# A graph layer and a ternary feed-forward network: the residual of nine tiles moved to GpSimd, and the first units' steps in another order

## The chip, the cores and the metric

One core of one Trainium2 chip runs the whole program. The metric is the device time of one execution in microseconds (us). The kernel before takes 344.32 us, the median of three runs (343.66 to 345.22). TensorE is called PE below, VectorE DVE, ScalarE ACT, GpSimd POOL and SyncE SP.

## The reference

```python
x = x + gnn(layernorm(x), src, dst, W_self, W_neigh, b)     # x: 1250 x 512
x = x + ffn(layernorm(x), w_gate, w_up, w_down)

def gnn(x, ...):      # 20000 edges, sorted by dst
    neigh = segment_sum(x[src], dst) / max(degree, 1)
    h = x @ W_self + neigh @ W_neigh + b
    h = where(h >= 0, h, 0.01 * h)
    return h / max(norm(h, axis=1), 1e-12)

def ffn(x, ...):      # weights ternary: sign times mean(|w|) of each group of 128
    h = silu(x @ gate.T) * (x @ up.T)                        # 1408 wide
    return h @ down.T
```

## The kernel before, in words

The 1250 nodes are ten tiles of 125 rows (`NT = 10`, `TP = 125`). Every engine runs a list of its own, in the order in which it is written, and they wait for each other by semaphores alone. There are three stages.

Stage 1 (to 112 us) normalizes x, multiplies it by the two weights, builds the 1250 x 1250 matrix of edge counts `a_t` from one-hot columns, and makes ternary signs of 25 of 34 blocks of weights.

Stage 2 is the loop `for n in range(NT)` on PE, DVE and ACT. PE adds up the neighbours of tile n in bank 4 + n % 2 (L1336: 20 products, `y_hi` and `y_lo` for each of ten source tiles). DVE takes the bank (`neighbour_sum`, L1121), applies the leaky slope (`leak`, L1127), and a tile later inverts the norm and adds the scaled tile to x (`residual`, L1130 to L1144, with the statistics for the second layernorm). ACT squares and sums the row (L876), takes the roots (L878, L831) and writes the normalized tile `xn` (`normalize1`, L837). PE transposes it after the sum n of tile n - 3 (L1349), ACT copies the result to `x1_hi` (L845), and DVE puts the rest into `x1_lo` (`x1_low`, L1157). Between these, ACT (`abs_of`, L768), POOL (`scales_of`, L658) and DVE (`ternary_of`, L987) make the signs of the last nine blocks: 4, 7, 4, 7, 4, 7 groups beside the tiles 0 to 5. POOL has first added the bias to all ten tiles (L698). `x1_lo` lies over `z`, the tiles that the residual reads.

Stage 3 is the feed-forward network in 33 units: one of 11 blocks of 128 hidden columns by one of three groups of tiles (376, 376 and 500 nodes). A unit has 12 pieces of two products each (L1405): G0 to G3 (gate), U0 to U3 (up), D0 to D3 (down); the D pieces follow three units behind (`LAG = 3`). Seven banks go round (`RING`): a piece waits until the piece seven before it has been taken. ACT takes G0, U0, D1 and D3 (L893), DVE the other eight (L1194). Silu is ACT's (L914), the product with up and the low part of h are POOL's (L721, L730). The eighth bank serves the transposes of signs (T) and of the tiles 7, 8 and 9 (X), at the places listed in `BANK7`. The signs of block f in use lie in `t_gu`, over the start of `a_t`, so that block 0 can't be written there before the last sum.

Of the kernel before, what the change touches and what calls it, by code (L numbers as in the profile page):

```python
# [27 lines left out]
F32R = mybir.dt.float32r  # L28
# [15 lines left out]
def gnn_ffn(nc, x, src, dst, w_self, w_neigh, bias, w_gate, w_up, w_down, out):  # L44
# [132 lines left out]
    eps = small("eps", [P, 1], F32)  # L177
    iota = small("iota", [P, 512], U16)
# [5 lines left out]
    tmp = small("tmp", [P, NCP], F32)  # L184
    flag = small("flag", [P, 1], I32)
# [22 lines left out]
    with ExitStack() as ctx:  # L208
# [134 lines left out]
        inv_done = sem("inv_done")  # L343
        x1_done = sem("x1_done")
# [11 lines left out]

        def down_jobs(n):

            lo, hi = (LOADS1 + max(0, min(NL, 3 * i // 2)) for i in (n, n + 1))
            return range(load_end[lo - 1], load_end[hi - 1])  # L360
# [42 lines left out]
        RING = [2, 6, 4, 5, 3, 1, 0]  # L403
# [18 lines left out]
        BANK7 = {(0, "U2"): ("T", 1, 0), (0, "U3"): ("X", 7), (1, "U2"): ("X", 8), (1, "U3"): ("T", 0, 1), (2, "U1"): ("X", 9),  # L422
# [10 lines left out]
        events = [("T", 0, 0)] + [BANK7[e] for e in sorted(BANK7)]  # L433
# [21 lines left out]
        t_done = sem("t_done")  # L455

# [159 lines left out]
        def _(pool):  # L616
# [79 lines left out]
            for t in range(NT):  # L696
                pool.wait_ge(z_out, t + 1)
                nc.gpsimd.tensor_tensor(z[:, t, :], z[:, t, :], bias_b[0:TP, :], ALU.add).then_inc(z_done, 1)  # L698
            for l in range(LOADS1, len(loads)):
                scales_of(l)  # L700

            nc.gpsimd.tensor_scalar(nscale[:], absum[:], 1.0 / P, Q_EPS, ALU.mult, ALU.add).then_inc(nscales, 1)
# [39 lines left out]
        def _(act):  # L742
# [105 lines left out]
            def ternary_out(f, down):  # L848
# [8 lines left out]
                if 2 <= f < NF - 1:  # L857

                    act.wait_ge(piece_ready, index[last_of[f - 2], "D0" if down else "U3"] + 1)
                if not down:  # L860
                    nc.scalar.activation(t_gu[:, t_slot[f], :, :].rearrange("p a d -> p (a d)"), source,  # L861
                                         ACT.Sign).then_inc(t_done, 1)
                else:
                    nc.scalar.activation(t_d[:, t_slot[f], :], source, ACT.Sign).then_inc(t_done, 1)


            for n in range(NT):
                if n == NT - 1:
                    act.wait_ge(n_ready, NT)
                    ternary_out(0, 0)  # L870
# [8 lines left out]
                if n >= 1:  # L879
# [14 lines left out]

            for n in range(NU + LAG):
                if n < NU:
# [7 lines left out]
                if n == 0:  # L904
                    normalize1(NT - 2)
                    ternary_out(1, 0)
                    x1_high(7)
# [7 lines left out]
                if n == 1:  # L915
                    x1_high(8)
                    normalize1(NT - 1)
                if n == 2:
                    x1_high(9)
                for what in ("D1", "D2", "D3"):  # L920
# [11 lines left out]
                    if what == "D2" and 1 <= n <= NU:  # L932
                        act.wait_ge(h_done, u + 1)
                        if u >= h_slots:
                            act.wait_ge(piece_ready, index[u - h_slots, "D0"] + 1)
                        nc.scalar.activation(h_hi[:, u % h_slots, 0:wu], hh_of(u), ACT.Copy).then_inc(hhi_done, 1)  # L936
                if n == 1:
                    ternary_out(0, 1)
                elif n in (3, 4) and (n, "U3") in BANK7:
# [14 lines left out]
        def _(dve):  # L954
# [175 lines left out]
            def residual(t, between=None):  # L1130
# [5 lines left out]
                if between is not None:  # L1136
                    leak(between)
                dve.wait_ge(inv_done, 2 * t + 2)
                nc.vector.scalar_tensor_tensor(out=x_sb[:, t, :], in0=z[:, t, :], scalar=inv[0:TP, t:t + 1],  # L1139
                                               in1=x_sb[:, t, :], op0=ALU.mult, op1=ALU.add).then_inc(x1_done, 1)  # L1140
                dve.wait_ge(x1_done, t + 1)
# [12 lines left out]
            def x1_low(t):  # L1154
                dve.wait_ge(xhi_done, t + 1)
                c, o, n = place_of(t)
# [3 lines left out]
            for n in range(NT):  # L1160
                neighbour_sum(n)
                if n >= 1:
                    residual(n - 1, between=n)
                else:
                    leak(n)
                if n >= 2:
                    shift1(n - 2)
                if n >= 3:
                    x1_low(n - 3)
                for j in down_jobs(n - 1):  # L1170
                    ternary_of(j)
                if n == 2:
                    inverse_degrees(DEG[2][0], DEG[2][1], 3, 2)
            shift1(NT - 2)
# [29 lines left out]
            for n in range(NU + LAG):  # L1204
                for what in TURN:
                    u = n - LAG if what[0] == "D" else n
                    if 0 <= u < NU and not by_act(u, what):
                        take(u, what)
                    if n == 1 and what == "U1":
                        shift1(NT - 1)  # L1210
# [7 lines left out]
                if n == 0:  # L1218
                    residual(NT - 1)
# [211 lines left out]
```

## Time and profile before

| | us |
|---|---|
| median of three runs | 344.32 |
| the profiled execution | 343.44 |
| its span in the trace | 341.7 |
| PE busy | 322.2 (94%) |
| DVE busy | 300.1 (88%) |
| ACT busy | 238.7 (70%) |
| POOL busy | 168.1 (49%) |

The span is what the trace covers, and 1.74 us of the profiled execution lie around it. Busy time is an average over the three stages. PE's first sum of stage 2 begins at 112.31 us, its first piece of stage 3 at 168.51 us.

### The profile page before, as it was taken

The numbers are of one execution on the slowest core, as the hardware profiler recorded it, in microseconds if no ns is written. First come the engines' busy times: TensorE is split into PE (matmuls) and PEld (weight loads), VectorE is DVE, ScalarE is ACT, GpSimd is POOL, SyncE is SP. The second block draws the span as 40 slices with busy tenths as digits, with TensorE's granted clock in tenths as the row PEclk, the third lists the DMA queues.
The fourth block names the chain that finished last, engine by engine and source line by source line (L and its number), as shares of the span: only waits on it lengthen the run. The fifth ranks groups of instructions, "written<-read, shape, count | busy, mean of one in ns | idle before, by whom it ended". The sixth has DMA issues, their size and how long they took to land.

```text
span 341.7 us, 5781 instructions
## 1 busy us (share of the span) xinstructions
PE 322.2 (94%) x1551; PEld 241.9 (71%) x1551; DVE 300.1 (88%) x782; ACT 238.7 (70%) x639; POOL 168.1 (49%) x234
## 2 busy tenths in 40 slices
PE   7999999999998999999969999999999999999991
PEld 3443545544543577777749898989989998899981
DVE  3899998998886348999799999999999999999993
ACT  2288987888985146784678876868768697676760
POOL 6034100000000870010006496889899897899992
PEclk9999999999999999999998999999999999999998
DMA  7982222132332002111001111111110100000305
GB/s 224 304 220 66 61 61 69 58 96 89 87 85 62 3 1 60 56 44 26 16 16 26 24 26 26 28 25 28 28 26 13 24 4 1 3 0 1 121 2 180
DMA packets 23550, 19.57 MB, mean 57 GB/s; under 512 B 15200, under 2 KB 16024, under 8 KB 23516
## 3 DMA queue, kind: packets, MB, share of 16 engines
q1 hardware_dynamic: 23438, 19.11, 20.1%
q8 instruction: 13, 0.21, 0.3%
q14 instruction: 21, 0.17, 0.1%
q10 hardware_dynamic: 78, 0.08, 0.1%
HBM read 13.73 MB, written 2.56 MB: 48 GB/s over the span
## 4 chain that ended last, share of the span: by engine, by line
PE 47%; DVE 13%; issue 4%; POOL 3%; ACT 1%; DVEq 0%; POOLq 0%; ACTq 0%
PE bank L1405 37%; PE bank L1336 6%; DVE tq_d L987 2%; POOL acc L711 2%; DVE bn L1142 2%; DVE x_sb L1139 2%; PE bank L1294 2%; DVE z L1121 1%; DVE z L1127 1%; DVE x_lo L1157 1%; PE bank L527 1%; PE bank L1322 1%; POOL h_lo L730 1%; DVE u_acc L1194 1%; DVE acc L1194 0%
## 5 line engine op out<-in xcount | busy, mean ns | idle before, releaser
L1405 PE MATMUL bank<-x_hi,t_gu 128*128 128x376 f32 (+1 forms) x264 | 94.7, 359 | 1.5 <-ACT t_gu L861 0.8
L1405 PE MATMUL bank<-x_lo,t_gu 128*128 128x376 f32 (+1 forms) x264 | 93.8, 355 | 0.0
L1294 PE MATMUL bank<-w_sb,xnT 128*125 128x512 f32 x160 | 83.0, 606 | 1.1 <-DMA w_sb<-in_L_gnn_W_neigh 0.6
L1194 DVE SCALAR_TENSOR_TENSOR g_acc<-bank,nscale,g_acc 128x376 f32<-128x376 f32 (+1 forms) x99 | 64.0, 647 | 4.6 <-PE bank L1405 3.6
L1194 DVE SCALAR_TENSOR_TENSOR u_acc<-bank,nscale,u_acc 128x376 f32<-128x376 f32 (+1 forms) x99 | 63.8, 645 | 0.0
L711 POOL TENSOR_TENSOR acc<-acc,d_one 128x376 f32<-128x376 f32 (+1 forms) x58 | 63.7, 1105 | 0.0
L658 POOL TENSOR_SCALAR thr<-absum 128x4 f32<-128x4 f32 (+1 forms) x34 | 9.1, 267 | 107.1 <-ACT mag_early L768 81.5
L721 POOL TENSOR_TENSOR hh<-sg,u_acc 128x376 f32<-128x376 f32 (+1 forms) x32 | 35.2, 1100 | 43.6 <-ACT sg L914 43.5
L1405 PEld LDWEIGHTS bank<-x_hi,t_gu 128*128 128x128 f32 x264 | 50.3, 191 | 6.3 <-issue 1.0
L1405 PEld LDWEIGHTS bank<-x_lo,t_gu 128*128 128x128 f32 x264 | 50.4, 191 | 3.4
L1246 PEld LDWEIGHTS bank<-hot_dst,hot_src 128*125 128x125 bf16 x157 | 20.7, 136 | 42.5 <-DVE hot_dst L1086 28.7
L1405 PE MATMUL bank<-h_hi,t_d 128*128 128x376 f32 (+1 forms) x132 | 47.4, 359 | 0.2
L1405 PE MATMUL bank<-h_lo,t_d 128*128 128x376 f32 (+1 forms) x132 | 46.6, 353 | 0.0
L1336 PE MATMUL bank<-y_hi,a_t 125*125 125x512 f32 x100 | 40.1, 401 | 0.8 <-DVE a_t L1043 0.8
L1194 DVE SCALAR_TENSOR_TENSOR acc<-bank,nscale,acc 128x376 f32<-128x376 f32 (+1 forms) x62 | 39.4, 643 | 0.3 <-PE bank L1405 0.3
L1336 PE MATMUL bank<-y_lo,a_t 125*125 125x512 f32 x100 | 39.5, 395 | 0.0
L730 POOL TENSOR_TENSOR h_lo<-hh,h_hi 128x376 fp32r<-128x376 f32 (+1 forms) x32 | 35.2, 1100 | 3.1 <-ACT h_hi L936 2.5
L893 ACT ACTIVATE d_one<-bank,nscale 128x376 f32<-128x376 f32 (+1 forms) x58 | 34.8, 604 | 1.7 <-PE bank L1405 1.7
L1086 DVE TENSOR_SCALAR hot_dst<-iota_w,key 128x140 bf16<-128x140 uint16 (+4 forms) x150 | 34.6, 272 | 1.2 <-PE bank L1246 1.1
L768 ACT ACTIVATE mag_early<-raw 128x128 f32<-128x128 f32 x99 | 29.6, 302 | 8.4 <-DVE tq_gu L987 6.7
L893 ACT ACTIVATE g_acc<-bank,nscale 128x376 f32<-128x376 f32 (+1 forms) x33 | 20.1, 608 | 16.5 <-PE bank L1405 15.8
L987 DVE SCALAR_TENSOR_TENSOR tq_gu<-mag_early,thr,raw 128x128 bf16<-128x128 f32 x88 | 28.8, 352 | 2.4 <-POOL thr L658 2.3
(142 smaller groups left out, 550.6 us busy)
## 6 DMA issues: line engine op xcount, KB each, us to landing
raw<-in_L_ffn_w_gate SPq DMA_DIRECT2D x11, 256.0 KB, 2.7
raw<-in_L_ffn_w_up SPq DMA_DIRECT2D x11, 256.0 KB, 2.6
out_x<-x_sb SPq DMA_DIRECT2D x10, 224.0 KB
raw<-in_L_ffn_w_down SPq DMA_DIRECT2D x8, 256.0 KB, 2.6
turned<-tq_gu SPq DMA_TRANSPOSE x80, 2.4
w_sb<-in_L_gnn_W_neigh SPq DMA_DIRECT2D x1, 1024.0 KB, 5.8
w_sb<-in_L_gnn_W_self SPq DMA_DIRECT2D x1, 1024.0 KB, 6.6
x_sb<-in_x SPq DMA_DIRECT2D x2, 448.0 KB
```

The lines of the kernel that those rows point to most:

```text
L711: nc.gpsimd.tensor_tensor(to, to, d_one[:, o, slot, 0:width(u)], ALU.add).then_inc(d_added, 1)
L721: nc.gpsimd.tensor_tensor(hh[:, u % 2, 0:w], sg[:, u % 2, 0:w], u_acc[:, u % 2, 0:w], ALU.mult).then_inc(h_done, 1)
L730: nc.gpsimd.tensor_tensor(h_lo[:, u % h_slots, 0:w], hh[:, u % 2, 0:w], h_hi[:, u % h_slots, 0:w].bitcast(F32), ALU.subtract).then_inc(hlo ...
L768: nc.scalar.activation(mag_of(j), raw_of(j), ACT.Abs, accum_out=absum[:, j:j + 1]).then_inc(abs_done, 1)
L893: nc.scalar.activation(to, bank_of(u, what)[:, 0:width(u)], ACT.Copy, scale=nscale[:, j:j + 1]).then_inc(act_took, 1)
L987: nc.vector.scalar_tensor_tensor(out=tq_of(j), in0=mag_of(j), scalar=thr[:, j:j + 1], in1=raw_of(j), op0=ALU.is_gt, op1=ALU.mult).then_inc ...
L1086: nc.vector.tensor_scalar(to, numbers, key[:, c:c + 1], None, ALU.is_equal).then_inc(hot_made, 1)
L1194: nc.vector.scalar_tensor_tensor(out=to, in0=bank_of(u, what)[:, 0:w], scalar=nscale[:, j:j + 1], in1=to, op0=ALU.mult, op1=ALU.add).then_ ...
L1246: nc.tensor.matmul(bank[k % 3][0:TP, 0:NT * WIN].rearrange("p (s d) -> p s d", d=WIN)[:, :, lo:hi], hot_src[:, c // SB % SBS, c % SB, 0:TP ...
L1294: last = nc.tensor.matmul(to[0:TP, :], xnT[:, t, k * TP:(k + 1) * TP], w_sb[:, k, half * D:(half + 1) * D], start=k == 0, stop=k == KD - 1)
L1336: last = nc.tensor.matmul(bank[4 + n % 2][0:TP, :], a_t[:, s, n * TP:(n + 1) * TP], y[:, s, :], start=s == 0 and y is y_hi, stop=s == NT - ...
L1405: last = nc.tensor.matmul(bank_of(u, what)[:, 0:width(u)], w, parts[h], start=h == 0, stop=h == 1)
```

## The change

Each part below is one of the edits.

- The residual of all tiles but tile 8 goes from one instruction of DVE to two of POOL: z times the inverse norm in place, then x plus z. POOL adds the bias to three tiles ahead of its loop and to tile t + 3 inside it; then come the scales of the tile's blocks of weights, and then the residual.
- DVE's loop has another order: `x1_low(n - 3)` comes first, then neighbour_sum, leak, the statistics of tile n - 1, the ternary groups, and only then the inverse norm of tile n and the shift of tile n - 1. `x1_low` also waits for the residual of the tile of `z` that it overwrites (`z_under`: tile 2 for the tiles 0 to 2, tile 5 for 3 to 5, 8 for 6, and 9 for 7 to 9).
- ACT normalizes tile n - 1 in its step n, after the absolute values, where it normalized tile n - 2 before them. At the last step it normalizes tile 8, copies tile 7 and takes the first two pieces before it squares tile 9.
- PE transposes tile n - 3 in the middle of the sum n. Tile 7 is transposed ahead of the first piece; the tiles 8 and 9 follow (2, G0) and (3, G0).
- The signs of block 0 go to `t_gu0`, over edge data that is no longer read. They are transposed after the sum of tile 7 and written in ACT's step 8.
- The ring of banks has another order, and in the units 0 to 2 tile 9's inverse norm, statistics, normalizing and the first h_hi have other places.

```diff
+    t_gu0 = place("t_gu0", [P, 2, D], F32R, "small", edge_data)
-        RING = [2, 6, 4, 5, 3, 1, 0]
+        RING = [2, 6, 4, 1, 0, 5, 3]
@@ pool
+            for t in range(3):
+                add_bias(t)
+            for t in range(NT):
+                if t + 3 < NT:
+                    add_bias(t + 3)
+                for l in down_loads_in(t):
+                    scales_of(l)
+                if l_done[t]:
+                    nc.gpsimd.tensor_scalar(nscale[:], absum[:], 1.0 / P, Q_EPS, ALU.mult, ALU.add).then_inc(nscales, 1)
+                if t != NT - 2:
+                    pool.wait_ge(inv_done, 2 * t + 2)
+                    nc.gpsimd.tensor_scalar(z[:, t, :], z[:, t, :], inv[0:TP, t:t + 1], None, ALU.mult).then_inc(h_unit, 1)
+                    pool.wait_ge(h_unit, min(t, NT - 2) + 1)
+                    nc.gpsimd.tensor_tensor(x_sb[:, t, :], x_sb[:, t, :], z[:, t, :], ALU.add).then_inc(x1_done, 1)
@@ scalar, in the loop over tiles
                 if n >= 3:
                     x1_high(n - 3)
+                if n == NT - 1:
+                    normalize1(NT - 2)
+                    x1_high(7)
+                    take_first()
...
-                if n >= 2:
-                    normalize1(n - 2)
...
                 for j in down_jobs(n):
                     abs_of(j)
+                if n == NT - 2:
+                    ternary_out(0, 0)
+                if 1 <= n < NT - 1:
+                    normalize1(n - 1)
+                if n == NT - 2:
+                    root_of(NT - 2)
@@ vector
             def x1_low(t):
                 dve.wait_ge(xhi_done, t + 1)
+                dve.wait_ge(x1_done, z_under(t) + 1)
...
             for n in range(NT):
+                if n >= 3:
+                    x1_low(n - 3)
+                if n == NT - 1:
+                    shift1(NT - 2)
                 neighbour_sum(n)
+                leak(n)
+                if 1 <= n < NT - 1:
+                    statistics1(n - 1)
                 for j in down_jobs(n - 1):
                     ternary_of(j)
+                if n < NT - 1:
+                    inverse_norm(n)
+                if 1 <= n < NT - 1:
+                    shift1(n - 1)
+                if n == NT - 2:
+                    residual(n)
+                    statistics1(n)
@@ vector, in the units
+                    if n == 0 and what == "G2":
+                        inverse_norm(NT - 1)
                     if n == 1 and what == "U1":
+                        statistics1(NT - 1)
+                        x1_low(7)
                         shift1(NT - 1)
-                if n == 0:
-                    residual(NT - 1)
-                    x1_low(7)
@@ tensor
+                    if s == NT // 2 and 3 <= n:
+                        t = n - 3
+                        if t >= 2:
+                            pe.wait_ge(xlo_done, t - 1)
+                        transpose_xn(t, normed1, x1_bank(t), x1n_T, place_of(t)[2])
...
-                if n == NT - 2:
+                if n == NT - 3:
                     pe.wait_ge(rdeg_done, 4)
                     ternary_in(0, 0)
...
+            through_bank7(("X", 7))
             for i, (u, what) in enumerate(pieces):
```

## Rows read from the trace of the kernel before

**Rows 1.** Chain that ended last, 112 to 190 us: start, us, what.
```profile
161.54 0.62 PE bank L1235 x4
...
162.61 4.71 PE bank L1336 x20
```
**Rows 2.** Waits of PE, 112 to 190 us: total, times, longest.
```profile
PE bank L1235 <- DVE x_lo L1157: 2.5, 1, 2.5
PE bank L1235 <- ACT xn L837: 1.2, 3, 0.5
```
**Rows 3.** Timeline of PE: start, us, instruction, idle before.
```profile
168.51 0.41 PE L1405 MATMUL bank<-x_hi,t_gu 128*128 128x376 f32 x1 [0.78 <-ACT t_gu L861]
...
178.74 0.51 PE L1405 MATMUL bank<-x_lo,t_gu 128*128 128x376 f32 x1
...
184.67 0.33 PE L1405 MATMUL bank<-h_hi,t_d 128*128 128x376 f32 x1
```
**Rows 4.** Timeline of DVE, one tile of stage 2.
```profile
146.33 0.74 DVE L1121 SCALAR_TENSOR_TENSOR z<-bank,rdeg,z 125x512 f32<-125x512 f32 x1
146.99 0.14 DVE L1133 TENSOR_SCALAR nrm<-nrm 125x1 f32<-125x1 f32 x1
...
147.25 0.67 DVE L1127 SCALAR_TENSOR_TENSOR z<-z 125x512 f32<-125x512 f32 x1
147.83 0.75 DVE L1139 SCALAR_TENSOR_TENSOR x_sb<-z,inv,x_sb 125x512 f32<-125x512 f32 x1
148.62 0.69 DVE L1142 BATCH_NORM_STATS2 bn<-x_sb 125x6 f32<-125x512 f32 x1
...
149.44 0.13 DVE L1149 RECIPROCAL rs<-sd 125x1 f32<-125x1 f32 x1
...
149.69 0.68 DVE L1157 TENSOR_TENSOR x_lo<-bank,x_hi 128x504 fp32r<-128x504 f32 x1
150.28 1.13 DVE L987 SCALAR_TENSOR_TENSOR tq_d<-mag_late,thr,raw 128x128 bf16<-128x128 f32 x4
151.32 0.75 DVE L1121 SCALAR_TENSOR_TENSOR z<-bank,rdeg,z 125x512 f32<-125x512 f32 x1
```
**Rows 5.** Timeline of ACT, the same tile.
```profile
147.95 0.60 ACT L876 ACTIVATE bank<-z 125x512 f32<-125x512 f32 x1 [0.47 <-DVE z L1127]
...
149.81 0.81 ACT L837 ACTIVATE xn<-x_sb,shift,rs 125x512 f32<-125x512 f32 x1
150.53 0.29 ACT L768 ACTIVATE mag_late<-raw 128x128 f32<-128x128 f32 x1
...
152.58 0.57 ACT L845 ACTIVATE x_hi<-bank 128x500 fp32r<-128x500 f32 x1
```
**Rows 6.** Groups of POOL by shape: busy us, mean ns, idle before.
```profile
L698 POOL TENSOR_TENSOR z<-z,bias_b 125x512 f32<-125x512 f32 x10 | 12.9, 1329 | 9.1 <-issue 9.1
...
L702 POOL TENSOR_SCALAR nscale<-absum 128x132 f32<-128x132 f32 x1 | 0.7, 698 | 0.1
...
L677 POOL TENSOR_SCALAR win_hi<-win_hi 128x157 f32<-128x157 f32 x1 | 0.6, 602 | 0.0
...
L625 POOL IOTA iota<- 128x512 uint16 x1 | 0.6, 559 | 0.0
```
**Rows 7.** Timeline of DVE and POOL where both work on SBUF.
```profile
118.10 1.12 DVE L1127 SCALAR_TENSOR_TENSOR z<-z 125x512 f32<-125x512 f32 x1
...
118.64 1.74 POOL L698 TENSOR_TENSOR z<-z,bias_b 125x512 f32<-125x512 f32 x1
```
**Rows 8.** Timeline of DVE, ACT and POOL, first units of stage 3.
```profile
172.25 0.61 DVE L1194 SCALAR_TENSOR_TENSOR g_acc<-bank,nscale,g_acc 128x376 f32<-128x376 f32 x1 [0.60 <-ACT g_acc L893]
...
177.81 1.28 ACT L914 ACT_TABLE_LOAD   x1
...
179.70 1.00 POOL L721 TENSOR_TENSOR hh<-sg,u_acc 128x376 f32<-128x376 f32 x1 [25.96 <-ACT sg L914]
```
**Rows 9.** Busy time of PE, PEld, DVE, ACT, POOL in a stretch, PE clock, DMA.
```profile
180.00:185.00 5.00, 5.00 (x26) 4.85 (x26) 4.65 (x10) 4.37 (x10) 2.89 (x4) 0.79 0.12 25
```

More of the change, by code:

```diff
@@ L177, in gnn_ffn @@
     eps = small("eps", [P, 1], F32)
+    edge_data = used["small"]
     iota = small("iota", [P, 512], U16)
@@ L343, in gnn_ffn @@
         inv_done = sem("inv_done")
+        h_unit = sem("h_unit")
         x1_done = sem("x1_done")
@@ L355, in gnn_ffn, with down_loads_in @@
         NL = len(loads) - LOADS1
+        def down_loads_in(n):
+            lo, hi = (LOADS1 + max(0, min(NL, 3 * i // 2)) for i in (n, n + 1))
+            return range(lo, hi)
         def down_jobs(n):
-            lo, hi = (LOADS1 + max(0, min(NL, 3 * i // 2)) for i in (n, n + 1))
-            return range(load_end[lo - 1], load_end[hi - 1])
+            ls = down_loads_in(n)
+            return range(load_end[ls.start - 1], load_end[ls.stop - 1])
+        l_done = [len(loads) - 1 in down_loads_in(n) for n in range(NT)]
         UNITS = [(0, 0), (0, 1), (1, 0), (1, 1), (0, 2), (1, 2)]
@@ L455, in gnn_ffn, with gate_up, z_under @@
         t_done = sem("t_done")
+        def gate_up(f):
+            return t_gu[:, t_slot[f], :, :] if f else t_gu0
+        def z_under(t):
+            c, o, n = place_of(t)
+            return (((C0[c] + CN[c]) * KD - CN[c] + o + n) * 4 - 1 - GAP) // (D * 4)
         def sg_of(u):
@@ L886, in _ @@
                     abs_of(j)
-            def take(u, what, to):
-                if took[u, what] == 1:
-                    act.wait_ge(nscales, 1)
-                act.wait_ge(piece_ready, index[u, what] + 1)
-                j = job_of(u, what)
-                nc.scalar.activation(to, bank_of(u, what)[:, 0:width(u)], ACT.Copy, scale=nscale[:, j:j + 1]).then_inc(act_took, 1)
+                if n == NT - 2:
[4 more added lines that the diff above has]
+                    root_of(NT - 2)
             for n in range(NU + LAG):
-                if n < NU:
+                if 0 < n < NU:
                     w = width(n)
@@ L931, in _ @@
                         ternary_out(*BANK7[n - 1, "U3"][1:])
[L932 to L937, printed above, removed]
+                    if what == "D2" and 2 <= n <= NU:
+                        high_of_h(u)
+                if n == 2:
                     ternary_out(0, 1)
+                    x1_high(9)
                 elif n in (3, 4) and (n, "U3") in BANK7:
@@ L1128, in leak, with inverse_norm @@
                                                op0=ALU.mult, op1=ALU.max).then_inc(leaky, 1)
-            def residual(t, between=None):
+            def inverse_norm(t):
                 dve.wait_ge(norms, t + 1)
@@ L1135, in residual @@
                 nc.vector.reciprocal(inv[0:TP, t:t + 1], nrm[0:TP, t:t + 1]).then_inc(inv_done, 1)
-                if between is not None:
-                    leak(between)
+            def residual(t):
                 dve.wait_ge(inv_done, 2 * t + 2)
@@ L1160, in _ @@
             for n in range(NT):
[L1161 to L1167, printed above, removed]
                 if n >= 3:
                     x1_low(n - 3)
+                if n == NT - 1:
+                    shift1(NT - 2)
+                neighbour_sum(n)
+                leak(n)
+                if 1 <= n < NT - 1:
+                    statistics1(n - 1)
                 for j in down_jobs(n - 1):
                     ternary_of(j)
+                if n < NT - 1:
+                    inverse_norm(n)
+                if 1 <= n < NT - 1:
+                    shift1(n - 1)
+                if n == NT - 2:
+                    residual(n)
+                    statistics1(n)
                 if n == 2:
                     inverse_degrees(DEG[2][0], DEG[2][1], 3, 2)
-            shift1(NT - 2)
             def take(u, what):
```

52 lines of the change are left out of this document (27 added, 25 removed).

## The prediction

> **What bounds the kernel now.** I read the chain of waits first. Between 112 and 161 us it runs mostly through DVE, and the sum of a tile on PE takes 4.71 us when it isn't held up [rows 1]. The transposes after it take 0.35 us more, so PE could do a tile in 5.06 us. The waits of PE come next: in stage 2 it waited three times for a normalized tile, 1.2 us in all (with the gaps that lie around these waits, 1.7 us), then 0.8 us for the signs of block 0 [rows 3], and 2.5 us for `x1_low` of tile 7 [rows 2]. From 184.67 us, the first D piece, to the tail its timeline shows no gap. So what the change can move is where that piece starts: the first G piece starts at 168.51 us, the first D piece at 184.67 [rows 3], and the rest of the program follows at PE's pace, untouched by the diff but for the names of the banks.
>
> The timeline of DVE says what a tile costs it in stage 2 [rows 4], start to start: sum 0.66, inverse norm 0.26, leak 0.58, residual 0.79, statistics 0.82, shift 0.25, `x1_low` 0.59, and 0.26 for each ternary group, 1.05 for four and 1.83 for seven. That is 5.0 and 5.8 us in turn, 5.4 in the mean: DVE, not PE, sets the pace of these tiles, and it never stands still between them.
>
> **What the change removes.** DVE loses 0.79 us a tile, which leaves it 4.2 and 5.0 us, under PE's 5.06. The 0.8 us for the signs goes, for they are ready before the last sum. Moving a transpose into the sum costs PE nothing more. If nothing else happened, the sums would end at 167.3 + 0.35 (tile 6's transposes now lie before that end) - 1.7 = 166.0 us, and the unit start would gain some 3 us more, because ACT takes the first two pieces ahead of tile 9's square. That is the ceiling: 4.5 us.
>
> **What it adds: a loop between DVE and ACT.** In the new order the last thing that DVE does for a tile is the shift; ACT's normalize waits for it (0.82 us), behind it on ACT stands `x1_high` (0.57 us) [rows 5], and the first thing of DVE's next step, `x1_low`, waits for that. Nothing of DVE can pass, the next `neighbour_sum` included. So DVE idles 0.82 + 0.57 and the handoffs, about 1.5 us, in every tile from 3 on, where it idled not at all. Its period becomes 4.2 + 1.5 = 5.7 and 5.0 + 1.5 = 6.5 us beside ternary groups, and 4.7 without. Before, `x1_low` stood behind the next tile's work, which hid ACT's part.
>
> **What it adds: POOL in the chain.** POOL starts the residual of tile n only after ACT's absolute values of the same tile, for the scales stand before it, and after DVE's inverse norm, which stands behind the ternary groups. From statistics(n - 1): 0.9, root 0.25, absolute values 4 or 7 by 0.293 = 1.2 or 2.05 (seven of them lie between 150.53 and 152.58) [rows 5], scales 0.2, scale z, add x. The add is 1.25 to 1.29 us by the bias adds [rows 6]. The multiply by a column of scalars is not in the trace. From the one-operation row, 157 columns in 0.60 us, with 0.2 us of it as the start of an instruction (what the four-column scales cost), it is 0.2 + 512 x 2.6 ns = 1.5 us; from the two-operation row, 132 columns in 0.70 us, 2.2 us [rows 6]; from below, a pass over 512 columns that reads nothing (iota) takes 0.56 [rows 6]. I take 1.5, the row with one operation. The leg is then 5.3 or 6.2 us with the handoffs, and not faster than the first loop.
>
> Beside POOL, DVE's passes with two SBUF inputs slow down: the leak at 118.10 took 1.12 us instead of 0.59, and the bias add under it 1.74 instead of 1.29 [rows 7, 4]. POOL was idle in stage 2 before, and is busy for 4 us of each tile now; I charge up to 0.5 us to each leak and add that meet, and as much again for the groups under a bias add. The Trainium skill has a rule that speaks against this change (GPSIMD Engine Reference, Key points): GpSimd shares its SBUF interfaces with VectorE, and contends with instructions that read two SBUF inputs. These two rows agree. The same page (Elementwise, side-by-side cycle accounting) has 512 elements of a tight one-input loop in 769 ns; the rows of 0.60 and 0.70 us for 157 and 132 columns are far from it. By that price my sum below would be 8.4 us instead of 11.0. Nothing else here uses it.
>
> **The two together.** `x1_low` of tile 0 now waits for the residual of tile 2, and that of tile 3 for the residual of tile 5, since it writes over them. There the legs do not overlap but follow each other, and tile 5's also has the 0.70 us of L702 in front. I wrote the four queues one below the other with these durations. The same done for the old order gives the end of the sums at 167.3, the first take of DVE at 172.2 and the first D piece at 184.2, against 167.34, 172.25 and 184.67 in the trace. For the new one:
> - Residual 2 ends at 138.9; `neighbour_sum` 3 can only start at 139.5, 4.6 us after its sum was ready.
> - PE's stalls: 0.4 us for that bank, then in the middle of the sums 5, 6 and 7 for normalized tiles 2, 3 and 4: 2.3, 1.9 and 1.8.
> - Residual 5 starts at 158.9, after nscale, and ends at 161.8; DVE has stood still since 157.0. PE loses 1.2 us for the bank and 2.3 for tile 5 in the sum 8.
> - Sum of the stalls 9.9 us, against 1.7: the sums end at 167.3 + 0.35 + 8.2 = 175.9.
> - Tile 7 is normalized only at 178.0, DVE's first take is at 181.9 (172.25 before [rows 8]): 9.7 us late.
> - Then eight takes of 0.52 and the inverse norm; statistics 9 wait for POOL to 186.7, ready 187.6; root 0.3, table 1.28 and silu 0.5 to 189.8; POOL's product 1.0 [rows 8]; two ACT takes, normalize 9 and h_hi to 192.6; POOL's h_lo and next product to 194.6; ACT's h_hi and the signs 1.1. First D piece 195.7, 11.0 us after the 184.67 of the trace.
>
> Here the change gives back nothing of what it lost; the silu of unit 0 now waits behind the root of tile 9, as it did, but the root waits for POOL. The rest keeps its length. 341.7 + 11.0 = 352.7 us of span, 354.4 with the 1.74 around it; the median of the runs lies 0.9 above the profiled execution, so I forecast 355.3. The ends: a multiply of 0.56 us gives 7.7 (352.0), one of 2.2 gives 15.2 (359.5).
>
> **Rivals.**
> - *POOL is always in time.* If the multiply is short and contention small, only the loop of DVE and ACT is left. Laid out the same way, without the waits of `x1_low` for residuals, without contention and with a short multiply of 0.8 us, the sums end at 169.4 and the first D piece at 188.8: 4.6 us, 348.9 us. For it: POOL has 5 us a tile. Against: it waits for the absolute values first.
> - *The clock falls.* After the 2.5 us stop before 178.08 us a product of 376 columns took 0.51 us instead of 0.33 [rows 3], and the granted clock was 0.79 in 180 to 185 us [rows 9]. Five stops of about 2 us in the sums, and one before the first piece, can do that again. In the sums the lateness of DVE hides most of it; at the sum 9 and the first units it does not: 2 to 4 us more, 358 us.
> - *The other side: faster.* If ACT has `x1_high` done before DVE comes to `x1_low`, DVE needs only 4.2 and 5.0 us a tile, PE sets the pace, and the ceiling of 4.5 us is had: 339.8. It decides at DVE's arrival at `x1_low`: its step must end over 1.5 us before the next sum is ready. With 5.06 us of PE and 5.0 of DVE in three of six tiles there is no such room, but the first tiles have some: the sums 0 and 1 end 7 and 5.7 us apart. If POOL then needed less than 1 us, the slack might last.
>
> **Chances.** The forecast 0.56 (its own range 351.5 to 359.5), POOL in time 0.16, the clock 0.15, faster 0.09, and 0.04 for gains and losses that cancel. Measurement can tell 0.5% here, 1.7 us: faster 0.09, same 0.04, slower 0.87. The range of 8 in 10 is 348 to 359.5 us.
>
> **What would show it.** In the profile after: idle time of DVE before L1157's line with ACT x_hi as its end, about 1.5 us a tile, and two longer ones (2.5 and 4.8 us) ended by POOL; PE idle in the middle of the sums 5 to 8, ended by ACT xn; POOL's multiply near 1.5 us; leaks of over 1 us; the last sum's end near 176 us. It is wrong if DVE's idle time before `x1_low` is under 0.5 us a tile, or if the sums end before 169 us.

## The result, and the profile after

The changed kernel takes 358.77 us, the median of four runs (358.03 to 360.55), against 344.15 us (343.66 to 345.22) for the kernel before in the same job: a ratio of 1.0428, interval 1.038 to 1.0475. The profiled execution took 359.23 us with a span of 357.5 us, 15.8 us more than before.

Three stretches make up the 15.8 us. From the first sum to the first D piece it is 85.7 us (113.30 to 198.99), against 72.4 (112.31 to 184.67): 13.3 us more. From there to the end of the span it is 158.5 us, against 157.0: 1.5 more. The first sum starts 1.0 us later, which tells nothing: the changed kernel and the eleven below, whose stage 1 is the same, start it between 112.05 and 115.83 us.

First the waits of stage 2 and of the first units, 112 to 215 us: total, times, longest.

```profile
PE bank L1288 <- ACT xn L869: 11.1, 7, 2.4
DVE x_lo L1204 <- ACT x_hi L877: 8.9, 6, 2.1
DVE x_lo L1204 <- POOL x_sb L734: 7.2, 2, 4.3
PE bank L1459 <- ACT t_d L896: 2.5, 1, 2.5
```

Before, DVE never waited at `x1_low`, and PE waited 1.2 us for normalized tiles [rows 2]. Now DVE stands still for 16.1 us before `x1_low`, and what it does next is late for PE. Of the 16.1 us, 14.2 lie in stage 2: 7.2 for POOL (tiles 0 and 3) and 7.0 for `x_hi` (tiles 1, 2, 4, 5 and 6). The sixth wait for `x_hi`, 1.92 us at 199.35, is tile 9's in the units; every kernel below that writes block 0's down signs in ACT's step 2 has it too, 1.91 or 1.92 us, so it has nothing to do with the loop. The timeline of DVE shows it tile by tile, where [rows 4] had a loop without a gap; the last column is the idle time before the instruction, and what ended it:

```profile
140.81 0.68 DVE L1204 TENSOR_TENSOR x_lo<-bank,x_hi 128x500 fp32r<-128x500 f32 x1 [2.97 <-POOL x_sb L734]
...
147.31 0.68 DVE L1204 TENSOR_TENSOR x_lo<-bank,x_hi 128x500 fp32r<-128x500 f32 x1 [2.07 <-ACT x_hi L877]
147.91 0.74 DVE L1163 SCALAR_TENSOR_TENSOR z<-bank,rdeg,z 125x512 f32<-125x512 f32 x1
148.68 1.29 DVE L1169 SCALAR_TENSOR_TENSOR z<-z 125x512 f32<-125x512 f32 x1
...
150.71 2.15 DVE L1029 SCALAR_TENSOR_TENSOR tq_d<-mag_late,thr,raw 128x128 bf16<-128x128 f32 x7
...
154.73 0.68 DVE L1204 TENSOR_TENSOR x_lo<-bank,x_hi 128x504 fp32r<-128x504 f32 x1 [1.36 <-ACT x_hi L877]
...
164.22 0.68 DVE L1204 TENSOR_TENSOR x_lo<-bank,x_hi 128x500 fp32r<-128x500 f32 x1 [4.28 <-POOL x_sb L734]
...
182.00 0.68 DVE L1204 TENSOR_TENSOR x_lo<-bank,x_hi 128x500 fp32r<-128x500 f32 x1 [0.84 <-ACT x_hi L877]
```

ACT shows the loop itself, normalize and then `x1_high`, at the time of the wait that ends at 147.31 (before: [rows 5]):

```profile
146.00 0.80 ACT L869 ACTIVATE xn<-x_sb,shift,rs 125x512 f32<-125x512 f32 x1
146.71 0.57 ACT L877 ACTIVATE x_hi<-bank 128x500 fp32r<-128x500 f32 x1
```

And POOL's timeline at tile 5, whose residual the wait of 4.28 us is for. The last scale (L677, three columns here) can't start before ACT's absolute values; the multiply (L732) stands behind it and behind `nscale`:

```profile
160.61 0.20 POOL L677 TENSOR_SCALAR thr<-absum 128x3 f32<-128x3 f32 x1 [0.67 <-ACT mag_late L800]
160.89 0.31 POOL L729 TENSOR_SCALAR nscale<-absum 128x132 f32<-128x132 f32 x1
161.18 1.57 POOL L732 TENSOR_SCALAR z<-z,inv 125x512 f32<-125x512 f32 x1
162.83 1.29 POOL L734 TENSOR_TENSOR x_sb<-x_sb,z 125x512 f32<-125x512 f32 x1
```

PE's timeline, with the stops in the middle of its sums, the end of the last one, and the first pieces (before: [rows 3]):

```profile
146.95 0.62 PE L1288 MATMUL bank<-ident,xn 126*128 126x126 f32 x4 [2.17 <-ACT xn L869]
...
154.36 0.62 PE L1288 MATMUL bank<-ident,xn 125*128 125x125 f32 x4 [2.15 <-ACT xn L869]
161.38 0.62 PE L1288 MATMUL bank<-ident,xn 125*128 125x125 f32 x4 [1.79 <-ACT xn L869]
165.61 0.50 PE L1394 MATMUL bank<-y_hi,a_t 125*125 125x512 f32 x1 [0.83 <-DVE z L1163]
170.43 0.62 PE L1288 MATMUL bank<-ident,xn 126*128 126x126 f32 x4 [2.24 <-ACT xn L869]
...
178.06 0.40 PE L1394 MATMUL bank<-y_lo,a_t 125*125 125x512 f32 x1
180.85 0.62 PE L1288 MATMUL bank<-ident,xn 125*128 125x125 f32 x4 [2.40 <-ACT xn L869]
...
185.86 0.44 PE L1459 MATMUL bank<-x_hi,t_gu 128*128 128x376 f32 x1 [1.57 <-ACT bank L925]
...
198.99 0.41 PE L1459 MATMUL bank<-h_hi,t_d 128*128 128x376 f32 x1 [2.52 <-ACT t_d L896]
```

The windows of the first units (us, then busy time and count of PE, PEld, DVE, ACT and POOL, then the granted clock, DMA share, GB/s); before, 185 to 200 us had a clock of 1.00 and PE busy throughout:

```profile
185.00:190.00 5.00, 4.14 (x15) 4.14 (x16) 4.52 (x11) 3.10 (x7) 2.86 (x2) 0.66 0.02 5
...
195.00:200.00 5.00, 2.30 (x14) 1.74 (x14) 3.08 (x7) 3.37 (x8) 2.92 (x3) 1.00 0.10 22
200.00:205.00 5.00, 5.00 (x21) 4.85 (x20) 4.35 (x9) 2.98 (x7) 1.98 (x2) 0.66 0.12 26
```

After PE's stops in the first units it runs a while at its lower level of 1.2 GHz: a product of 376 columns takes 0.52 us there in place of 0.33. The second such stretch lies behind the first D piece:

```profile
200.26 0.47 PE L1459 MATMUL bank<-h_lo,t_d 128*128 128x376 f32 x1
200.53 0.52 PE L1459 MATMUL bank<-x_hi,t_gu 128*128 128x376 f32 x1
...
203.66 0.37 PE L1459 MATMUL bank<-h_hi,t_d 128*128 128x376 f32 x1
```

Between 200.26 and 203.66 us eleven products start, in 3.40 us; at the 0.17 us from one to the next that stands before and after this stretch they would have taken 1.9.

### The profile page after: what moved, and what is told of

Same layout as the page of the kernel before. It is cut to its first block, busy times and chain, and to the rows that moved or that the text cites. A ratio compares the mean times of both kernels' runs of the same rounds, so it can differ in the third digit from the quotient of the medians.

```text
span 357.5 us, 5798 instructions
## 1 busy us (share of the span) xinstructions
PE 325.7 (91%) x1551; PEld 243.3 (68%) x1551; DVE 297.2 (83%) x773; ACT 237.9 (67%) x639; POOL 193.0 (54%) x252
## 3 DMA queue, kind: packets, MB, share of 16 engines
HBM read 13.73 MB, written 2.56 MB: 46 GB/s over the span
## 4 chain that ended last, share of the span: by engine, by line
PE 47%; DVE 8%; ACT 6%; POOL 5%; issue 4%; DVEq 0%; ACTq 0%; POOLq 0%
PE bank L1459 40%; PE bank L1394 3%; ACT mag_late L800 2%; DVE z L1169 2%; DVE z L1163 1%; PE bank L1347 1%; POOL z L732 1%; DVE tq_d L1029 1%; ACT bank L925 1%; POOL x_sb L734 1%; POOL acc L743 1%; ACT x_hi L877 1%; DVE bn L1188 1%; PE bank L1437 1%; PE bank L546 1%
## 5 line engine op out<-in xcount | busy, mean ns | idle before, releaser
L677 POOL TENSOR_SCALAR thr<-absum 128x4 f32<-128x4 f32 (+1 forms) x34 | 7.9, 232 | 101.3 <-ACT mag_early L800 82.9
L1299 PE MATMUL bank<-hot_dst,hot_src 128*125 128x140 bf16 (+6 forms) x157 | 27.6, 258 | 4.2 <-DVE hot_dst L1128 4.2
```

What stands on the lines that cost most here:

```text
L677: nc.gpsimd.tensor_scalar(thr[:, js], absum[:, js], 0.5 / P, 0.5 * Q_EPS, ALU.mult, ALU.add).then_inc(scales, 1)
L1299: nc.tensor.matmul(bank[k % 3][0:TP, 0:NT * WIN].rearrange("p (s d) -> p s d", d=WIN)[:, :, lo:hi], hot_src[:, c // SB % SBS, c % SB, 0:TP ...
```

## The experiments

Eleven kernels, all made from the changed one, were timed in three jobs, in which the kernel before took 344.82, 344.93 and 344.48 us. The last three columns are of the profiled execution. They are differences of four times: the start of the first sum, the end of the last, the first product with `t_d`, the end of the span. Kernels of different jobs are compared by their medians; the medians of the kernel before, in the four jobs, differ by up to 0.8 us, so a difference across jobs of less than that says nothing.

| kernel | median us (runs) | ratio to before, interval | first to last sum | first sum to first D | from there to the end |
|---|---|---|---|---|---|
| before | 344.15 (4) | | 55.0 | 72.4 | 157.0 |
| changed | 358.77 (4) | 1.0428 (1.038 to 1.0475) | 65.2 | 85.7 | 158.5 |
| xlow_late | 354.53 (4) | 1.0274 (1.0227 to 1.0321) | 62.4 | 81.4 | 158.6 |
| res_first | 359.55 (4) | 1.0427 (1.0355 to 1.05) | 66.9 | 85.8 | 158.7 |
| res_dve | 356.01 (4) | 1.0334 (1.0288 to 1.038) | 60.8 | 81.9 | 158.7 |
| both_orders | 351.38 (4) | 1.0185 (1.0139 to 1.0231) | 58.4 | 76.3 | 159.9 |
| good_order_dve | 348.15 (10) | 1.01 (1.0064 to 1.0136) | 57.2 | 74.9 | 157.2 |
| signs_early | 357.28 (6) | 1.034 (1.0288 to 1.0393) | 65.2 | 84.4 | 158.2 |
| dve_reordered | 346.51 (10) | 1.0047 (1.0021 to 1.0074) | 54.7 | 72.7 | 158.6 |
| candidate | 343.35 (10) | 0.9955 (0.9923 to 0.9987) | 54.7 | 69.8 | 158.3 |
| passes_two_inputs | 355.0 (4) | 1.0344 (1.0273 to 1.0415) | 64.5 | 82.2 | 157.3 |
| passes_one_input | 351.47 (4) | 1.0194 (1.0153 to 1.0235) | 60.6 | 78.2 | 159.7 |
| good_order_units | 345.0 (10) | 1.0025 (1.0009 to 1.0042) | 57.3 | 72.1 | 158.6 |

**xlow_late: the loop alone.** `x1_low` goes behind the statistics; everything else, POOL's residual too, stays.

```diff
-                if n >= 3:
-                    x1_low(n - 3)
 ...
                 if 1 <= n < NT - 1:
                     statistics1(n - 1)
+                if n >= 3:
+                    x1_low(n - 3)
```

> The changed kernel with one edit: x1_low(n - 3) behind the statistics of tile n - 1, no longer first in DVE's step; the residual stays on POOL. Theory A (two loops, DVE to ACT to DVE, and POOL's leg behind the absolute values): the first loop is gone, the second is left: 4 to 5 us less than the 358.8 of the changed kernel, near 354; DVE no longer idle before x1_low with ACT's x_hi as its end, but idle before the statistics, ended by POOL. Theory B (what costs is POOL's slow residual and its contention, whatever the order): within 1 us of 358.8. Theory C (the transposes in the middle of the sums ask for the tiles half a sum too early): PE's waits for ACT's xn stay near 11 us, 357 or more.

It came as expected, 4.2 us under the changed kernel. The waits for `x_hi` in the loop, 7.0 us, are all gone (the one of 1.9 us that is left is tile 9's in the units). In their place DVE waited for POOL, at the statistics, in eight tiles:

```profile
DVE bn L1188 <- POOL x_sb L734: 14.1, 8, 3.1
DVE x_lo L1204 <- ACT x_hi L877: 1.9, 1, 1.9
```

So the second loop was hidden behind the first, and is nearly as long. A third reading, that PE asks too early for the tiles because it now transposes them in the middle of the sums, had set 357 us or more here. It is out, and dve_reordered below, which keeps these transposes, needs 54.7 us for its sums where the kernel before needs 55.0.

**res_first: POOL's leg alone.** On POOL the residual goes ahead of the scales, on DVE the inverse norm ahead of the ternary groups.

```diff
@@ pool, in the loop over t
+                residual of t (two instructions)
                 for l in down_loads_in(t):
                     scales_of(l)
 ...
-                residual of t
@@ vector
+                if n < NT - 1:
+                    inverse_norm(n)
                 for j in down_jobs(n - 1):
                     ternary_of(j)
```

> The changed kernel with the other half: POOL does the residual of tile t ahead of the scales of its blocks, and DVE inverts the norm ahead of the ternary groups; x1_low stays first in DVE's step. Theory A: POOL's leg is shorter by the absolute values (1.2 or 2.05 us) and the groups, residual 5 ends 5 us earlier, the loop between DVE and ACT is left: 354 again (4 to 5 us less). Theory B: less than 1 us of gain. Theory C: 357 or more.

A miss: 359.55 us, no gain at all. The wait for POOL at `x1_low` is gone, but the one for `x_hi` has grown to 12.0 us in eight tiles, seven of them in the loop with 10.1 us. So 4.1 of the 14.2 us of waits are won. The ternary groups, which POOL's passes now lie beside, take 3.35 to 3.39 us for seven, where the changed kernel has 1.89 to 2.15; the 33 instructions together take 14.8 us in place of 9.7, and these 5.1 us eat what was won. The number is that of theory B, but xlow_late has shown that the order counts too: both are at work.

**both_orders.** Both edits together.

> Both edits together, everything else as in the changed kernel, the residual of nine tiles on POOL included. Theory A: neither loop is left, DVE needs 4.2 or 5.0 us a tile, PE sets the pace; the sums end 10 us earlier than in the changed kernel: 343.5 to 345.5, level with the kernel before or up to 0.5 us better; more than the two edits' gains apart, because the loops stood beside each other. Theory B: 356 or more, for POOL's work and its contention are all there. Theory C: 355 or more.

Both loops are open now and DVE doesn't wait for `x_hi` in the loop at all, but 351.38 us is still some 7 us above what I expected. The ternary groups again take most of it: 3.38, 2.27 and 3.61 us for seven, against 1.91 three times in good_order_dve. In 128 to 166 us the 33 ternary instructions of both_orders take 13.7 us, the same 33 of good_order_dve 9.1:

```profile
L1029 DVE SCALAR_TENSOR_TENSOR tq_d<-mag_late,thr,raw 128x128 bf16<-128x128 f32 x33 | 13.7, 480 | 0.0
```
```profile
L1024 DVE SCALAR_TENSOR_TENSOR tq_d<-mag_late,thr,raw 128x128 bf16<-128x128 f32 x33 | 9.1, 343 | 0.0
```

**res_dve and good_order_dve: the residual back on DVE**, in the changed kernel's order and in that of both_orders.

```diff
@@ pool
-                if t != NT - 2:
-                    residual of t (two instructions)
@@ vector, res_dve
                 if n < NT - 1:
                     inverse_norm(n)
+                if n < NT - 1:
+                    residual(n)
@@ vector, good_order_dve: neighbour_sum(n), leak(n), residual(n - 1), statistics1(n - 1),
@@ x1_low(n - 3), inverse_norm(n), ternary groups, shift1(n - 1)
```

> The changed kernel with the residual of all tiles on DVE again, behind the inverse norm of the same tile; POOL has the bias and the scales alone; x1_low stays first in DVE's step. Theory A: the loop between DVE and ACT is left with 0.8 us more in DVE's step: 355 (3 to 4 us less than the changed kernel). Theory B: all of the loss was POOL's, so 345. Leaks back at 0.67 us each, where POOL's contention is what made them 1.2 to 1.6.

> both_orders with the residual of all tiles on DVE again; the rest of DVE's order (statistics, x1_low, inverse norm, ternary groups, shift) is the same, so this pair differs by what POOL does alone. both_orders took 351.4, 7 us more than expected, and its 7 ternary groups took up to 3.6 us instead of 1.9. Theory A2 (POOL's two passes slow DVE's two-input instructions beside them, and this gives back what taking 0.8 us off DVE saves): the groups take 1.1 and 1.9 us again, DVE's step is 5.0 or 5.8 us, and the time is 348 to 350, below both_orders. Theory D (moving the residual to POOL is a gain in the right order, and both_orders lost its 7 us in the first units): 352 or more, since DVE has 0.8 us more in every tile.

good_order_dve came as expected; res_dve gained 2.8 us where 3 to 4 were expected, and its leaks are all back at 0.69 us. In res_dve the loop of DVE and ACT stands alone: `x1_low` waits 8.8 us for `x_hi` in seven tiles of the loop (10.7 with tile 9's), and it costs 356.0 - 348.15 = 7.9 us against the other order. In the good order POOL's residual costs 351.38 - 348.15 = 3.2 us, though it takes 0.74 us a tile from DVE.

**passes_two_inputs and passes_one_input: POOL's passes by themselves.** To good_order_dve two passes of POOL are added in each of six tiles. They write a scratch buffer, and the one thing that waits for them is ACT's copy of tile 6, which comes 12 us after the last of them, so that they can only get in the way. In passes_one_input the second pass is the multiply once more.

```diff
+                if t < 6:
+                    pool.wait_ge(inv_done, 2 * t + 2)
+                    pool.wait_ge(h_unit, 2 * t)
+                    nc.gpsimd.tensor_scalar(noise[:], bias_b[0:TP, :], inv[0:TP, t:t + 1], None, ALU.mult).then_inc(h_unit, 1)
+                    pool.wait_ge(h_unit, 2 * t + 1)
+                    nc.gpsimd.tensor_tensor(noise[:], noise[:], bias_b[0:TP, :], ALU.add).then_inc(h_unit, 1)
```

> good_order_dve (residual on VectorE; 348.15 us), to which six pairs of GpSimd passes are added that nothing depends on but one late x1_high: in each of the first six tiles, after the inverse norm, a multiply of 125 x 512 numbers by a column and an add of two 125 x 512 tensors, into a scratch buffer. No instruction of VectorE or ScalarE waits for them (x1_high of tile 6 does, long after the last), so the residual's route has no hand-over in it. Theory (GpSimd's passes slow VectorE's instructions that read two tensors from SBUF): ternary groups that lie beside them go from 1.91 to 3.0 to 3.6 us for seven and from 1.12 to 1.3 to 1.5 for four, leaks reach 1.3 to 1.5 us more often, and as VectorE sets the pace, time goes to 351 to 354 us. Rival (both_orders was 3.2 us slower than good_order_dve because statistics and normalize wait for GpSimd): nothing changes, 347.8 to 348.8.

> As passes_two_inputs, but the second pass is another multiply by a column (one tensor read from SBUF) in place of the add. If only GpSimd's instructions with two tensor inputs hold up VectorE, groups and leaks keep their durations (1.91, 1.12 us) except beside the bias adds, and the time is 348 to 349 us. If every pass of GpSimd does it, which the group of four at 141.51 in both_orders speaks for (1.48 us with only a multiply beside it, 1.12 without), groups of seven take 2.7 to 3.4 us, and the time is 350.5 to 353.5. I expect the latter.

The rival had forecast no change, and as the main cause it is out: passes that nobody has to wait for cost 6.8 us (355.0 - 348.15), with a multiply in place of the add 3.3 us. The first lies 1 us over the range that I had set, the second inside its own, and the groups of seven took 3.87 to 3.99 us in the one, 2.25 to 3.44 in the other. (The test doesn't weigh how much the hand-over adds in both_orders: DVE waits there twice for POOL at the statistics, 1.7 us in all.) The timeline of DVE, and then of POOL, in passes_two_inputs shows what happens:

```profile
139.55 1.68 DVE L1173 SCALAR_TENSOR_TENSOR z<-z 125x512 f32<-125x512 f32 x1
141.16 1.77 DVE L1186 SCALAR_TENSOR_TENSOR x_sb<-z,inv,x_sb 125x512 f32<-125x512 f32 x1
142.96 0.69 DVE L1192 BATCH_NORM_STATS2 bn<-x_sb 125x6 f32<-125x512 f32 x1
```
```profile
139.40 1.29 POOL L736 TENSOR_TENSOR noise<-noise,bias_b 125x512 f32<-125x512 f32 x1
140.64 1.73 POOL L720 TENSOR_TENSOR z<-z,bias_b 125x512 f32<-125x512 f32 x1
```

They take turns. The leak (0.69 us when alone) starts at 139.55 under an add that ends at 140.69, and ends 0.54 us after that. POOL's bias add starts at 140.64, but ends 1.14 us after the leak's end at 141.23, so it had to wait for it (1.29 alone, 1.73 here). The residual starts at 141.16 and ends 0.56 us after the bias add. The Trainium skill says this (SBUF — State Buffer, SBUF: two separate sides): of the two engines the one that starts first has the shared ports for its whole instruction, and the other blocks. For the adds these rows agree.

Not every instruction of DVE is held up. The statistics (0.695 us in the mean, 0.695 without the passes), the sum (0.751, 0.751) and `x1_low` (0.662, 0.660) kept their times; the first reads one tensor, the other two read one of theirs from PSUM. And the multiply doesn't hold on for its length: in both_orders six ternary instructions start between 134.5 and 136.2 us, under or just before a multiply of 1.58 us (the list of that line: least, median and longest duration in ns), and the longest takes 0.78 us; the add behind it holds one for 1.38:

```profile
L1029 DVE SCALAR_TENSOR_TENSOR tq_d<-mag_late,thr,raw x6: 331/342/778, 134.5 to 136.2; 128x128 bf16<-128x128 f32 x6
L1029 DVE SCALAR_TENSOR_TENSOR tq_d<-mag_late,thr,raw x3: 341/343/1378, 136.0 to 136.5; 128x128 bf16<-128x128 f32 x3
```

There the rule of the Trainium skill and the rows differ, and the rows decide; why the multiply lets go stays open.

So the 3.3 us of passes_one_input aren't simply the price of its multiplies. They also move the bias adds, which come behind them, onto other instructions of DVE. The longest ternary instruction there, 1.43 us, lies beside a bias add from 161.63 to 162.91 us. And the shift, one column wide, is held for 1.12 us under another; it too reads two tensors from SBUF:

```profile
135.24 1.28 POOL L720 TENSOR_TENSOR z<-z,bias_b 125x512 f32<-125x512 f32 x1
```
```profile
135.42 1.12 DVE L1201 SCALAR_TENSOR_TENSOR shift<-mv,rs 125x1 f32<-125x1 f32 x1
```

How the 3.3 us divide between the two isn't shown.

**signs_early, dve_reordered, candidate and good_order_units: the first units.** signs_early is the changed kernel with the signs of block 0 of the down projection written in ACT's step 1 of stage 3 and not in step 2, where they stand behind the second h_hi. dve_reordered has the residual on DVE and a third order; candidate is dve_reordered with the early signs and with tile 9's residual, statistics and `x1_low(7)` at the end of unit 0; good_order_units is good_order_dve with the same two edits.

```diff
@@ scalar, in the units (signs_early, candidate, good_order_units)
                 if n == 1:
                     x1_high(8)
+                    ternary_out(0, 1)
                 if n == 2:
-                    ternary_out(0, 1)
                     x1_high(9)
@@ vector, in the units (candidate, good_order_units)
                     if n == 1 and what == "U1":
-                        statistics1(NT - 1)
-                        x1_low(7)
                         shift1(NT - 1)
+                if n == 0:
+                    residual(NT - 1)
+                    statistics1(NT - 1)
+                    x1_low(7)
@@ vector, in the loop (dve_reordered, candidate): statistics1(n - 1), neighbour_sum, leak,
@@ x1_low(n - 3), ternary groups, inverse_norm(n), residual(n), shift1(n - 1)
```

> The changed kernel with one edit in the units: ACT writes the down signs of block 0 (t_d) in its step 1, before it needs anything of unit 1, not in step 2 behind h_hi of unit 1. The first D piece waited for them 2.5 us, with h_lo ready 2.1 us before. Theory A: 1.5 to 3.5 us less than the changed kernel (2.0 of the wait and a part of what the fall of the clock after it cost), 355 to 357. Rival: the wait goes to h_lo or to the ring of banks and less than 0.7 us is won.

> Residual on DVE, in the order statistics(n - 1), sum, leak, x1_low(n - 3), ternary groups, inverse norm(n), residual(n), shift(n - 1): the statistics fill the time in which DVE waits for the next sum, and x1_low stands behind the sum, where ACT has long been ready. Units as in the changed kernel. Theory A: sums end within 1.5 us of where they end in the kernel before; total 346 to 348, the rest of the loss being in the first units. Rival: with 5.0 and 5.8 us of DVE the sums end as in good_order_dve and the time is the same as its within 1 us.

> dve_reordered with two edits in the units: the signs early as in signs_early, and tile 9's residual, statistics and x1_low of tile 7 at the end of unit 0 as in the kernel before, so that the root of tile 9, and the table load and silu of unit 0 behind it, come 2 us earlier. Theory A: 2 to 4 us less than dve_reordered, 342.5 to 344.5, level with the kernel before or 0.5% better. Rival: the ring of banks or DVE's takes bound the first units, less than 1 us.

> good_order_dve (348.15 us) with the first units' steps put back in two places: block 0's signs of the down projection go back to ScalarE's step 1, and tile 9's residual, statistics and x1_low(7) to the end of unit 0 on VectorE. Of the whole change it then has left: row 0's early signs, the transposes inside the sums, and VectorE's order. Theory (the new order of the first units costs about 3 us, by the candidate 3.2): 344.5 to 346 us, no different from the kernel before. Rival (the two edits helped the candidate only because its sums ended early): 347.5 to 348.5.

The signs alone gave 1.5 us in the median, the least that I had expected, with a time 0.3 us over the expected 355 to 357; as the two kernels ran in different jobs, that is weak evidence by itself. dve_reordered came as expected, with 54.7 us for the sums and 346.51 in all. Both edits gave 3.2 us in the candidate (346.51 to 343.35) and again 3.15 in good_order_units (348.15 to 345.0), so the gain doesn't hang on when the sums end. Where it comes from stands in ACT's timeline of good_order_dve and of good_order_units, whose sums end 0.4 us apart:

```profile
180.40 0.29 ACT L858 ACTIVATE sd<-mv,eps 125x1 f32<-125x1 f32 x1 [1.81 <-DVE mv L1185]
...
187.78 0.61 ACT L891 ACTIVATE t_d<-turned 128x512 fp32r<-128x512 bf16 x1
```
```profile
179.77 0.29 ACT L858 ACTIVATE sd<-mv,eps 125x1 f32<-125x1 f32 x1 [0.79 <-DVE mv L1185]
...
182.27 0.62 ACT L891 ACTIVATE t_d<-turned 128x512 fp32r<-128x512 bf16 x1
```

The root of tile 9, with the table and the first silu behind it, comes 9.5 us after the sums' end in the one and 8.5 in the other; the signs come 5.9 us sooner on that count, and the stop of PE for them, 2.51 or 2.52 us in every kernel made from the changed one that has them in step 2, is gone; what stands before the first D piece is 0.27 us for a take of DVE.

candidate is the one kernel that beats the one before, by 0.45% (interval 0.13 to 0.77%), at the limit of what can be told. It keeps the residual on DVE.

## Why the prediction was right, and where its sizes were off

The direction and the mechanism held: slower, with 355.3 us forecast, 358.77 measured, inside the range of 348 to 359.5. That it lies inside is partly luck. The upper end was worked out for a multiply of 2.2 us; the multiply took 1.57, near the 1.5 of the forecast, and other terms filled the room. The time is also nearer to the 358 us of the clock rival than to the forecast.

- **The loop of DVE and ACT.** Forecast 1.5 us a tile from 3 on; measured 1.35 or 1.36 in tiles 2, 4 and 5, with 2.07 in tile 1, 0.84 in tile 6 and 7.0 us in the five tiles together. xlow_late and res_dve show that it is real and that it isn't the only one.
- **POOL in the chain.** Forecast waits of 2.5 and 4.8 us before `x1_low` of tiles 0 and 3; measured 2.97 and 4.28. The multiply was taken as 1.5 us from a row of 157 columns [rows 6]; it is 1.57. The Trainium skill's figure for a tight loop (GPSIMD Engine Reference, Elementwise — side-by-side cycle accounting), 769 ns for 512 elements, on which nothing rested, is half of that. `nscale`, counted at 0.70 us, took 0.31.
- **PE's stops.** Forecast 0.4, 2.3, 1.9, 1.8, 1.2 and 2.3 us, 9.9 in all. Measured 0.77, 2.17, 2.15, 1.79, 0.83 and 2.24: 9.95.
- **The end of the sums** should have come at 175.9 - 112.3 = 63.6 us after the first product; it came at 65.2, though the stops are the same. Here a term was missing: the time lost around a stop. The prediction's own figure for the old order was 1.7 us for waits of 1.2, so 0.17 us for each of three; six stops at that rate are 1.0 of the 1.6 us. The timeline of PE has it in the gap before a stopped transpose:

```profile
133.05 0.59 PE L1288 MATMUL bank<-ident,xn 125*128 125x125 f32 x4
133.40 0.47 PE L1394 MATMUL bank<-y_hi,a_t 125*125 125x512 f32 x1
...
144.39 0.39 PE L1394 MATMUL bank<-y_lo,a_t 125*125 125x512 f32 x1
```

  From 144.39 to the transposes at 146.95 it is 2.56 us: 0.23 from one product to the next, the wait of 2.17, and 0.16 more. The transposes behind a stop then take 0.38 us, where those at 133.05, without one, take 0.35. The other 0.6 us come from smaller things: a seventh stop, which the forecast didn't have (0.17 us for the transposes at 138.46, and 0.17 around it), 0.03 to 0.05 for each of five transposes behind a stop, and 0.1 for the product that restarts the sum at 142.20 (0.33 us to the next in place of 0.23). That is 0.6.
- **The first units** were laid out as 19.8 us from the sums' end to the first D piece, and took 20.5. I had the signs behind the second h_hi, rightly, but not the stop of 1.57 us for the bank of tile 9's square, nor the fall of the clock behind it (186.5 to 189.8 us, where eleven products take 1.4 us more than at the full clock). How much of the 0.7 us is theirs isn't separated: the signs, on which the D piece waits, come by way of tile 9's residual on POOL, DVE and ACT.
- **The clock** stood among the rivals, at 2 to 4 us more, and should have been in the sum: 0.66 in two windows of the first units. Behind the first D piece the eleven slow products shown above account for 1.5 us by themselves, and the other kernels bear it out. Where it stayed at 1.00 with the same units (good_order_dve, passes_two_inputs), the stretch after the first D piece is 157.2 and 157.3 us; where it fell in that stretch (changed, xlow_late, res_first, res_dve, dve_reordered), 158.5 to 158.7. (candidate and good_order_units have a clock of 1.00 there and still 158.3 and 158.6. Of three short waits for takes, 0.28, 0.44 and 0.26 us in the candidate, two lie after their first D piece, with 0.7 us; signs_early, with 158.2, has the same two. The other 0.3 to 0.7 us stay open. In both_orders and passes_one_input the clock had fallen before that piece, and the stretch is 159.9 and 159.7.)
- **Contention** was charged at up to 0.5 us for each leak that meets an add. In the changed kernel that was nearly enough, three leaks of 1.2 to 1.58 us in place of 0.69, because the ternary groups lie before the inverse norm, while POOL waits. The forecast missed what the Trainium skill's rule means here: not a slower instruction but a turn waited for, up to an add's length each time. That is why a better order of the same parts (res_first) gained nothing, which I had expected to gain 4 to 5 us. (The 0.59 us that the prediction sets against a leak of 1.12 is the time from its start to the next start; the leak's own duration in the kernel before is 0.67.)

The forecast in sum: 11.0 us of span, measured 15.8. The 4.8 are 1.0 for the start of the first sum, 1.6 in the sums, 0.7 in the first units, and 1.5 for the clock. In the medians only 3.5 us are missing, and that is luck again: the forecast put the median 0.9 us over the profiled execution, as in the kernel before, and here it lies 0.5 under it.

The 14.6 us of the whole change can be taken apart roughly by the medians, in this order: 7.4 for the two loops (changed to both_orders), 3.2 for POOL's residual in an order without them, 3.15 for the two steps of the first units, and 0.5 for what is left (good_order_units against before), which holds the transposes in the sums, row 0's early signs, the rest of DVE's order and the ring of banks. The four add up to 14.3; the 0.3 that are missing are what the kernel before itself differs by between the first job and the last. In another order the parts would come out otherwise, since the loops and POOL's passes stand beside each other. The first units cost these 3 us even where nothing else was late; the prediction had set a gain of some 3 there in its ceiling. No run shows that gain: in good_order_dve, with neither the loops nor POOL's residual, the first D piece comes 17.7 us after the last sum's end, and in the kernel before 17.4 us after it.

## What to carry to other kernels

When an engine is relieved of an instruction, follow the instruction's result and not the engine's busy time: here 0.79 us a tile was saved on DVE, and 0.8 to 4.3 us a tile came back as waits at the head of its queue. A step that needs another engine's answer belongs behind work that covers the answer's way, never first in the list. And GpSimd isn't a free engine beside a busy VectorE: where both read two tensors from SBUF, count on a wait of up to the other's whole instruction at each meeting, and lay GpSimd's passes beside instructions that read one tensor, or one of their two from PSUM. A pass of GpSimd with one tensor is cheaper, not free: it pushes the passes behind it onto other instructions.

## What the runs showed of the hardware

- An add of GpSimd over 125 x 512 holds a VectorE instruction with two SBUF inputs until the add ends: up to 1.43 us for a ternary instruction of 0.34 (passes_one_input), up to 1.83 us for a leak of 0.69 (res_first). It works both ways: GpSimd's add went from 1.29 to 1.73 us in the rows above. A multiply by a column held one for 0.78 us at most in the stretch above. VectorE's instructions with one tensor in SBUF kept their times beside both.
- GpSimd needs 1.57 us for a multiply of 512 columns by a column of scalars, 1.29 for an add of two tensors: the operation with one tensor input is the slower one. Beside a busy VectorE the multiply, too, went up, to 2.07 us in passes_two_inputs. Two dependent instructions of it, the multiply and the add, stand 0.08 to 0.09 us apart.
- The 0.70 us of `nscale` [rows 6], from which the prediction's upper end for the multiply was worked out, was most likely no price but a turn waited for: it started at 153.05 under a residual of DVE that ends at 153.57. In the changed kernel DVE stands still meanwhile, and the same instruction takes 0.31.
- A stop of PE in the middle of a sum cost 0.15 to 0.18 us beside its idle time, at each of seven places in the changed kernel.
